# Last attention of a gated two-layer decoder block: a maximum tile as eight matmuls of 64 rows by 32 columns instead of two of 64 rows by 128 columns

## The reference, cut to what matters

```python
qkv = (x @ W_qkv).reshape(Bx, Nx, 3, H, D)
q, k, v = (qkv[:, :, 0], qkv[:, :, 1], qkv[:, :, 2])
...
logits = jnp.einsum('bqhd,bkhd->bhqk', q * scale, k)
def masked_attn(tok_mask):
    key_mask = jnp.concatenate([jnp.ones((Bx, REG), bool), tok_mask], axis=1)
    l = jnp.where(key_mask[:, None, None, :], logits, -jnp.inf)
    a = jax.nn.softmax(l, axis=-1)
    return jnp.einsum('bhqk,bkhd->bqhd', a, v)
```

## Time and profile before

| | us |
|---|---|
| median of 3 runs | 1279.92 (1279.77 to 1280.38) |
| the profiled execution, its own time | 1277.68 |
| its span, first to last instruction | 1275.6 |
| TensorE busy over the span | 1195.5 (94%) |
| VectorE busy | 973.4 (76%) |
| ScalarE busy | 818.6 (64%) |
| TensorE matmuls, as many weight loads | 10370 |

### The profile page before, as it was taken

One profiled execution on the slowest core, in us unless ns is written; L12 is line 12 of the kernel. 1 busy time (PEld: TensorE's weight loads), 2 busy tenths in 40 slices (PEclk: granted clock), 3 DMA queues, 4 the chain that ended last, 5 costly groups with the idle time before them and its releaser, 6 DMA issues.

```text
span 1275.6 us, 26127 instructions
## 1 busy us (share of the span) xinstructions
PE 1195.5 (94%) x10370; PEld 549.2 (43%) x10370; DVE 973.4 (76%) x1431; ACT 818.6 (64%) x1471; POOL 257.4 (20%) x200
## 2 busy tenths in 40 slices
PE   4888997999999899988999999999999999999998
PEld 2566784555558446444233323232332323232345
DVE  4896586565536758667999999999999999999912
ACT  1324564577761563213888888888888888888872
POOL 2130443455661242370000000000000000000000
PEclk8879996799999999998999999999999999999999
DMA  6100227456510234453255443554345443555014
GB/s 197 28 1 1 38 60 124 79 118 127 89 39 1 72 130 126 131 70 53 57 88 94 68 95 64 100 101 74 82 81 95 89 83 72 99 87 87 12 41 138
DMA packets 89960, 101.71 MB, mean 80 GB/s; under 512 B 22122, under 2 KB 60268, under 8 KB 89840
## 3 DMA queue, kind: packets, MB, share of 16 engines
q1 hardware_dynamic: 89840, 100.06, 38.7%
HBM read 71.47 MB, written 24.33 MB: 75 GB/s over the span
## 4 chain that ended last, share of the span: by engine, by line
PE 59%; DVE 30%; ACT 3%; issue 2%; SPq 2%; DMA 1%; POOL 1%; POOLq 0%; DVEq 0%; ACTq 0%
DVE sm L2187 23%; PE ps L1658 10%; PE ps L1649 9%; PE ps L1636 7%; PE ps L1425 3%; PE ps L1519 2%; PE ps L1416 2%; PE ps L1417 2%; PE ps L1719 2%; PE ps L1478 2%; PE ps L1381 1%; PE ps L1383 1%; PE ps L1434 1%; PE ps L1539 1%; DVE XN L1795 1%
## 5 line engine op out<-in xcount | busy, mean ns | idle before, releaser
L2187 DVE TENSOR_REDUCE sm<-ps 128x1 f32<-128x1024 f32 x512 | 602.0, 1219 | 34.0 <-PE ps L1636 29.9
L1127 ACT ACTIVATE W<-ps 128x512 f32<-128x512 f32 x1024 | 535.0, 604 | 123.4 <-PE ps L1658 121.0
L1658 PE MATMUL ps<-R 99*32 99x512 bf16 x4096 | 317.5, 384 | 0.9
L1649 PE MATMUL ps<-W,R 128*32 128x512 f32 x2048 | 265.4, 594 | 0.0
L1658 PEld LDWEIGHTS ps<-R 99*32 99x32 bf16 x4096 | 85.1, 94 | 203.6 <-ACT W L1127 156.3
L1636 PE MATMUL ps<-R 50*128 50x512 bf16 x512 | 91.0, 390 | 12.6 <-DVE sm L2187 8.3
L1050 ACT ACTIVATE R<-ps 77x512 f32<-77x512 f32 x128 | 75.2, 592 | 32.2 <-PE ps L1417 24.2
L1636 PE MATMUL ps<-KM,R 50*128 50x512 bf16 x512 | 88.7, 384 | 5.2 <-DVE sm L2187 0.2
L878 POOL COPY R<-R 128x512 f32<-128x512 f32 x16 | 9.7, 611 | 385.5 <-PE ps L1649 385.5
L1649 PEld LDWEIGHTS ps<-W,R 128*32 128x32 f32 x2048 | 62.9, 111 | 45.8 <-issue 0.5
L1960 DVE TENSOR_REDUCE small<-ps 128x4 bf16<-128x308 f32 x128 | 57.4, 473 | 24.0 <-PE ps L1383 23.9
(11 more groups left out here) (259 smaller groups left out, 1506.4 us busy)
## 6 DMA issues: line engine op xcount, KB each, us to landing
R<-x_parts SPq DMA_DIRECT2D x96, 128.0 KB, 4.8
R<-q_parts SPq DMA_DIRECT2D x192, 64.0 KB
R<-q_parts SPq DMA_DIRECT2D x96, 128.0 KB
R<-k_parts SPq DMA_DIRECT2D x96, 128.0 KB
x_parts<-R SPq DMA_DIRECT2D x8, 768.0 KB, 5.6
q_parts<-R SPq DMA_DIRECT2D x24, 256.0 KB, 2.6
k_parts<-R SPq DMA_DIRECT2D x24, 256.0 KB, 2.6
X<-in_x SPq DMA_DIRECT2D x4, 1024.0 KB, 10.3
```

The lines of the kernel that those rows point to most:

```text
L1127: act.activation(PR[:, s % 2, h, :], third_bank("score", 64 * u + n), ACT.Exp, scale=0.25).then_inc(s_sfree, 1)
L1649: mm = pe.matmul(bank(7)[32 * h:32 * h + 32, :], VST[j][:, k, h, :], PR[:, s % 2, h, :], start=(k == 0), stop=(k == TB - 1))
L1658: mm = pe.matmul(o[32 * c:32 * c + 32, :], KST[j][0:MAX_ROW + 1, h, t:t + 32], QST[j][0:MAX_ROW + 1, h, 512 * (s // 8):512 * (s // 8) + 51 ...
L2187: dve.tensor_reduce(MX[:, half, h, q:q + 1], bank(2 * ((p + 1) % 2), 2), AX, ALU.max).then_inc(s_tfree, 1)
```

## The change

`max_tile` makes the same 128 by 1024 logits with the same operands, but splits the 128 query columns in four strips of 32 and gives each strip and each half of the keys its own matmul. The strip's place among the columns is also its place among PSUM's partitions. The semaphore is still incremented once, by the last of the eight.

```diff
                 pl = take_pair(p)
                 q, h = a // 4, a % 4
-                for i in range(2):
-                    v = slice(64 * i, 64 * i + MROWS)
-                    mm = pe.matmul(pl[:, 512 * i:512 * i + 512], QMH[j][h][v, P * q:P * q + P], KM[j][v, h, :],
-                                   start=True, stop=True)
+                for c in range(4):
+                    t = P * q + 32 * c
+                    for i in range(2):
+                        v = slice(64 * i, 64 * i + MROWS)
+                        mm = pe.matmul(pl[32 * c:32 * c + 32, 512 * i:512 * i + 512], QMH[j][h][v, t:t + 32],
+                                       KM[j][v, h, :], start=True, stop=True)
                 mm.then_inc(s_turn, 1)
```

## The result

The changed kernel took 1288.15 us in the median of 5 runs (1285.30 to 1291.53), the kernel before 1279.92 (1277.24 to 1280.38): 0.7% slower, ratio 1.0070 with a 95% interval of 1.0052 to 1.0089. The forecast was 1285 in a range of 1268 to 1310. Its profiled execution took 1288.22 us, with a span of 1286.5, 10.9 more than the span of before. Of these, 1.4 us lie ahead of the first maximum tile, where the programs are the same (the first reduce starts at 541.69 instead of 540.29), so they are scatter between executions. 9.1 lie between the second transpose and the last (604.3 to 1216.4 before, 605.7 to 1226.9 after), the steady part, and 0.4 around it.

The account below looks back on a forecast made before the run. A loop of TensorE tiles and VectorE reduces, 5.01 us per two steps, was taken to bound the kernel. Profiled 1277.7 plus 5.0 for later starts is 1282.7; the runs' median lies 2.2 above, so 1285 us, range 1268 to 1310.

Parts of the forecast that it names:

- The loop of tile B, tile A and two reduces: Steady part: two steps every 5.01 us, 2.505 a step against TensorE's own 2.38, so the loop sets the pace.
- ScalarE isn't near: Stretch of 580 us: exponentials take 476 us, with 95 us idle, so ScalarE doesn't set the pace.
- The price of a change of shape: Tile B to score group and score group to tile A: 0.10 us each, kept although columns become equal.
- the first rival of the prediction: Both loop places lose 0.10: 24 us less, 1256; one direction spared, 12 us, 1268. Chance 0.12 for both cases.
- The longer tile: Each maximum tile's last matmul starts and ends 21 ns later, bounds 0 and 42; 5.0 us together.
- The start term: Six further matmuls side by side in a tile, at 3.5 ns each: 21 ns.
- enter the loop twice: The 21 ns delay tile A's reduce and the score group behind tile B: loop from 5.01 to 5.05 us.
- The eight do run side by side: Rival 4 said they don't: a tile takes 0.22 us longer, 76 us more, 1356. Chance 0.07.
- TensorE bound by instructions: Rival 3: 40 matmul records a step instead of 28 bind TensorE; 1351 at 70 ns each, 1495 at 85. Chance 0.11.
- A fixed price for bringing a matmul: Rival 3's form: one matmul with its load costs up to 85 ns to bring; from 63 ns it decides.
- the rival's other sign: Rival 3 in the changed profile: VectorE well under 90% busy.
- the likeliest stretch: The forecast's own case for the time: 1282.5 to 1290 us, chance 0.50.

Follow-up runs that it names:

- moving8: Kernel before, with each of the tile's two matmuls cut into four of 128 moving columns, no strips: 1281.96 us, ratio 1.0029.
- half64: Kernel before, with only half of each tile made, by four matmuls of 50 rows by 32 columns on the identity: 1287.13 us, one execution.
- strips64: Kernel before, with the tile made by four matmuls, two strips of 64 columns by two halves of the keys: 1283.20 us, ratio 1.0034.
- moving16: Changed kernel, with each of the tile's eight matmuls cut into two of 256 moving columns, sixteen a tile: 1299.94 us, one execution.
- half128: Kernel before, with half tiles by four matmuls of 114 rows (not 50) by 32 columns on the identity: 1261.48 us, one execution.

## Why the prediction was right, point by point

The terms of the loop, as medians over the steady part, in ns, taken from single records (some 80 to 130 tiles for each number, more in half128), for loops without a transpose. "Side by side" is how many matmuls of a tile run at once; "end to reduce" is from the last matmul's recorded end to the reduce's start.

| kernel | matmuls a tile, side by side | waiting tile B to next tile A | tile A to reduce | of it end to reduce | loop |
|---|---|---|---|---|---|
| before | 2, 2 | 2163 | 432 | 42 | 5008 |
| moving8 | 8, 2 | 2170 | 439 | 42 | 5024 |
| half64 | 4, 4 | 2167 | 448 | 51 | 5026 |
| strips64 | 4, 4 | 2180 | 462 | 52 | 5054 |
| changed | 8, 8 | 2180 | 482 | 72 | 5072 |
| moving16 | 16, 8 | 2182 | 484 | 72 | 5077 |
| half128 | 4, 4 | 1957 | 441 | 51 | 4810 |

The loop is the sum of the two terms, two reduces (1141 from the first's start to the second's, and the second's 1215, the same in all) and 54 to 58 from VectorE's end to tile B. Read directly, from a tile A's reduce to the fourth reduce after it, the median is within 3 ns of it in every kernel.

**What bounds the kernel: right, but not in all loops.** The loop of tile B, tile A and two reduces explains every variant: the table's loops follow from its terms. The prediction took the loops as equal, with 0.3 us on top in eight steps for the transpose. Read one by one, the four loops of eight steps were 5.01, 5.01, 5.07 and 5.21 before. The last is the transpose's, 0.21 more. The third is the one in which ScalarE makes a copy besides its exponentials, and a score group waits for it. So "ScalarE isn't near" holds for its busy share and not for this loop.

**The price of a change of shape stays: right.** The rows-only place of the earlier trace rows was the right thing to read. half128 shows what its loss would have been worth: 216 ns against half64 in the loops that VectorE bounds, but only 18.8 us over the steady part, where the first rival of the prediction had 24, because ScalarE comes in.

**The longer tile: the mechanism right, a size off.** The start term, 3.5 ns a matmul and 21 in all, measured 20 (a tile's first start to its last, 3 before and 23 after), and behind tile B it cost 17. But the step that said the 21 ns "enter the loop twice" missed the larger part of the term at VectorE: the reduce comes 50 ns later, not 21. Beside the late start there are 30 ns between the last matmul's end and the reduce, and the table shows what they go by: 42 with two side by side, 51 with four, 72 with eight, whether the tile has eight matmuls or sixteen, and still 42 with eight that run two at a time. That is 5 ns for each further one. The Trainium skill has this in TensorE: Matmul & The Clock Gate, section The cost: per-tile semaphore tail, with 4.7 ns a tile; by it six more are 28 ns, an estimate, and these runs agree with 30. I had used the section ahead of it and not this one. What happens in these 30 ns no run here shows. So a loop costs 64 ns more (17, 50, and 3 less before tile B) instead of 42. With the change the four loops of eight steps are 5.07, 5.07, 5.08 and 5.28: three pay 64 or 65 ns, the one with the transpose among them, and the third, in which there was a wait for ScalarE before, pays 17. That makes 0.21 us: 6.2 us in all, where the prediction had 5.0. Two errors partly cancel in that sum, the 22 ns missing in a loop and the quarter of the loops that pays little.

**The rivals.** The shape's price going away didn't happen. The eight do run side by side. TensorE bound by instructions is half of a miss. A fixed price for bringing a matmul, the form in which I wrote it, doesn't come near to binding: moving16 excludes 62 ns. But the number of instructions does cost, in a way that I hadn't thought of and that the sum put at nothing: their packets come late when the loads of the stacks are ahead of them. That is 3.1 us, shown by taking the loads away and borne out by the packets' times. The prediction gave idle time that ends by "issue" between matmuls of one shape as a sign of this rival, and said that the forecast is wrong if spacing between equal shapes changes at all. At 940 us it did, 0.86 instead of 0.22; the rival's other sign, VectorE well under 90% busy, did not come (92%).

**The sum.** 6.2 + 3.1 = 9.3 in the profiled steady part, where 9.1 to 9.5 were read; by the medians 8.2 (6.7 to 11.4 by the interval). The forecast was 5, from 0 to 10. So the loop's part was foreseen within a quarter, and that the time still fell into the likeliest stretch, 1282.5 to 1290, is in part the width of that stretch: a third of the loss has a cause that the prediction didn't have.

**Open.** Why some units are spared, although their loads are the same, wasn't followed, nor what makes the clock fall in the prologue of one execution and not of another. With one profiled execution of each kernel, the split into 6.2 and 3.1 rests on single traces; the medians only agree with it.

## What to carry to other kernels

Cutting a matmul into narrow strips that run side by side is free in streaming time but not in latency: each further matmul beside the others made the reduce start some 8 ns later here (3.3 for its start, 5 at its end), and it bought nothing, because the neighbours differ in the number of rows, and that alone is a change of shape at 0.10 us. In a kernel whose engines wait for each other in a loop, count latencies around the loop, not busy shares: 64 ns in 5 us were 0.5%. When you fill a wait with work, look for the second loop of the same kind and for the engine that is next (ScalarE, once the rows were equal), and count instructions too where large transfers share the DMA engines with the instruction packets.

## What the runs showed that I had not expected

- The reduce starts 42, 51 and 72 ns behind the last recorded end of 2, 4 and 8 matmuls that run side by side.
- A weight load of 64 columns takes 103 ns, of 32 columns 89, of 128 columns 93.
- TensorE's instructions come in packets of 16 KB. With 1.61 MB of other transfers in 13.2 us ahead of a packet, TensorE ran dry at one packet every 8 us (up to 0.9 us, 3.1 us over the run), and not at one every 11 us.
- 56 matmul records and as many loads ran in a 2.7 us step, 48 ns each, with the spacing of equal shapes unchanged.
- TensorE went on 1.3 to 1.8 us behind the end of an instruction packet in every one of these stalls that was looked at.
- The prologue's stretch between two transposes took 24.9 to 28.7 us, longer the lower its granted clock (0.89 to 0.66 over 580 to 610 us), in no order of the kernels.
